# A recommendation tower on one core: plain fp32 field products on 32-row strips, weights loaded once, and gathers without a pause between them

## The reference

```
e = jnp.stack([tbl_0[ids[:, 0]], ..., tbl_38[ids[:, 38]]], axis=1)   # 512 x 39 x 32
z = jnp.einsum('bpc,apc,bpa->bp', e[:, ROW, :], w, e[:, COL, :])     # 512 x 741 pairs
h = jnp.concatenate([z, dense_ctx], axis=1)                          # 512 x 757
h = jnp.maximum(h @ W_top1 + b_top1, 0.0)                            # 512 wide
h = jnp.maximum(h @ W_top2 + b_top2, 0.0)                            # 256 wide
y = h @ W_top3
```

## Time and profile before

| | |
|---|---|
| time, median of 3 runs | 290.9 us (290.44 to 292.17) |
| profiled execution: span from first to last instruction | 285.0 us |
| the median over that span | 5.9 us more |
| busy: PE, DVE, POOL, ACT | 198.8, 146.6, 134.8, 97.5 us |
| mean granted TensorE clock | 0.844 of full speed |

### The profile page before, as it was taken

How to read it: one execution, slowest core, us unless ns; L and a number is a source line. 1 busy time by engine, 2 the same in 40 slices (tenths; PEclk the granted TensorE clock), 3 DMA queues, 4 the chain that set the end, 5 groups by cost and what they waited for, 6 DMA issues and landing times.

```text
span 285.0 us, 2687 instructions
## 1 busy us (share of the span) xinstructions
PE 198.8 (70%) x974; PEld 73.5 (26%) x974; DVE 146.6 (51%) x115; ACT 97.5 (34%) x142; POOL 134.8 (47%) x134
## 2 busy tenths in 40 slices
PE   0048668453212277738798197699899999999996
PEld 0012223000000033213333032243333334344341
DVE  0353794101000027824794266389599779898230
ACT  2516899300000047830540071037127127110032
POOL 7774767777777300776587887200042015007000
PEclk9999797755555559795999669599999999999999
DMA  4869779700000003997266018148715846450000
GB/s 134 257 210 300 285 177 212 164 16 13 14 13 13 9 0 74 300 207 148 50 158 166 12 41 183 41 96 167 167 33 118 183 98 129 98 121 1 0 2 0
DMA packets 11352, 31.40 MB, mean 110 GB/s; under 512 B 3230, under 2 KB 7098, under 8 KB 10379
## 3 DMA queue, kind: packets, MB, share of 16 engines
q1 hardware_dynamic: 7882, 29.45, 42.1%
q0 software_dynamic: 3456, 1.78, 3.5%
HBM read 12.34 MB, written 0.00 MB: 43 GB/s over the span
## 4 chain that ended last, share of the span: by engine, by line
PE 51%; issue 18%; DMA 9%; DVE 7%; SPq 6%; another core or an unknown queue 4%; ACT 3%; DVEq 0%; ACTq 0%
PE t_ps L719 16%; PE z_ps L735 15%; PE z_ps L688 9%; DMA mlp<-tbl 6%; PE side_ps L750 5%; DMA wring<-w_lo 4%; DVE prod L658 3%; SPq L425 2%; PE t_ps L777 2%; DVE prod L629 2%; SPq L431 1%; SPq L475 1%; PE t_ps L765 1%; PE t_ps L770 1%
## 5 line engine op out<-in xcount | busy, mean ns | idle before, releaser
L658 DVE TENSOR_TENSOR prod<-t_ps,eT 128x1536 f32<-128x1536 f32 (+2 forms) x70 | 109.9, 1600 | 79.3 <-PE t_ps L719 49.7
L514 POOL DMA_INDIRECT gathered<-tbl,ids_sb x108 | 104.9, 971 | 53.5 <-issue 31.4
L719 PE MATMUL t_ps<-stack,wring 128*128 128x512 f32 x210 | 72.9, 464 | 12.2 <-issue 6.7
L735 PE MATMUL z_ps<-prod,sel 128*32 128x512 f32 x380 | 57.5, 645 | 4.6 <-issue 4.6
L719 PEld LDWEIGHTS t_ps<-stack,wring 128*128 128x128 f32 x210 | 38.3, 205 | 65.8 <-issue 39.5
L688 PE MATMUL z_ps<-prod,room 125*32 125x512 bf16 x72 | 21.0, 534 | 34.1 <-issue 33.3
L528 POOL TENSOR_TENSOR room<-room,w_hi 128x512 f32<-128x512 f32 x3 | 3.9, 1286 | 66.3 <-ACT w_hi L603 66.3
L629 DVE TENSOR_SCALAR prod<-mlp,slice_rows 125x2048 bf16<-125x2048 f16 x18 | 14.8, 856 | 23.0 <-remote 23.0
L587 ACT ACTIVATE stack<-hi_lo 32x512 fp32r<-32x512 f32 x39 | 24.6, 629 | 2.6 <-issue 1.2
L580 ACT ACTIVATE stack<-eT 32x512 fp32r<-32x512 f32 x39 | 24.4, 625 | 1.0 <-PE t_ps L719 0.7
L750 PE MATMUL side_ps<-room,mlp 128*128 128x512 f32 x32 | 18.4, 660 | 7.7 <-ACT eT L567 7.6
(11 more groups left out here) (49 smaller groups left out, 113.5 us busy)
## 6 DMA issues: line engine op xcount, KB each, us to landing
wring<-w_hi SPq DMA_DIRECT2D x30, 224.0 KB
wring<-w_lo SPq DMA_DIRECT2D x30, 224.0 KB
stack<-stack SPq DMA_DIRECT2D x9, 512.0 KB
w_lo<-wst SPq DMA_DIRECT2D x4, 896.0 KB, 15.2
eT<-hot_ids SPq DMA_DIRECT2D x3, 1024.0 KB
gathered<-tbl,ids_sb POOLq DMA_INDIRECT x108
mlp<-w SPq DMA_DIRECT2D x1, 1536.0 KB
mlp<-tbl SPq DMA_DIRECT2D x12, 125.0 KB
```

The costliest lines, as they stand in the source:

```text
L514: pool.indirect_dma_start(gathered[:, n % GATHER_BUFS, b, K * r:K * r + K], None, tables[f], bass.IndirectOffsetOnAxis(ap=ids_sb[:, F * b ...
L658: dve.tensor_tensor(prod[:, g % XSLOTS, 0:n, :], t_ps[g % 2][:, 0:n, :], field, ALU.mult).then_inc(multiplied, 1)
L719: mm = pe.matmul(t_ps[g % 2][:, i, :], wring[:, c % WSLOTS, passes % WCHUNK, :].bitcast(F32R), stack[:, J % STACKS, src - G * J, :].bitcas ...
L735: mm = pe.matmul(z_ps[K * (u % G):K * (u % G) + K, :], sel[:, u // G, :], prod[:, g % XSLOTS, t - TILE_BASE[g], :], start=(u < G), stop=(u ...
```

## The change

- **Tiles in plain fp32.** No high and low parts, no `stack`, no weight ring. A tile of field r of block J is a full fp32 product that uses only the 32 rows of that field, `w_sb[rows, w_tile, :]` by `eT[rows, J, :]`; the four tiles of a *quad* (J, I) use the four row strips 0, 32, 64 and 96 of the array and four PSUM banks. Within a block (the diagonal) two tiles of 64 rows each are used, for the last block one of 128. The count stays at 190 tiles, now in 55 quads and 100 *pairs* of one or two tiles; DVE multiplies a pair at a time. `t` has three slots of two banks, `prod` six slots.
- **Weights loaded once.** `w_sb` holds all of the weights; SP issues all its loads at the start, the table blocks first, then `w_sb` block by block, then the network's weights.
- **Byte-wise lookups.** The twelve looked-up fields are now blocks 0, 1 and 2. The upper 16 bits of each fp32 entry are read in place as bf16; ACT turns the two lower bytes into bf16 (two copies a block). The products of the upper half and of the two lower bytes go to two banks, and ACT writes them back as the two halves of the fp32 word. There are still 12 products a slice and 24 slices. The ids are spread over the partitions by 12 small PE products instead of three 1 MB loads. `hot` has six buffers of its own.
- **Gathers.** Seven buffers, one for each gathered block (3 to 9), so POOL issues all 108 without a wait or other work in between.
- The early part of the first layer takes 5 of the 6 z blocks in three rounds (20 full products), the sixth comes last.

```diff
+LOOKED = [0, 1, 2]
+DIAGONAL = [[(0, 1), (0, 2), (1, 3)], [(2, 1), (3, 0), (3, 2)]]
+for _J in range(NBLK):
+    QUADS += [(_J, _I, FIELDS_IN[_J]) for _I in range(_J)]
+    QUADS.append((_J, _J, 2 if FIELDS_IN[_J] == G else 1))
+PAIRS = [(q, i, min(2, QUADS[q][2] - i)) for q in range(NQUAD) for i in range(0, QUADS[q][2], 2)]
+TSLOTS = 3
+XSLOTS = 6
+ROUNDS = [[0, 1], [2, 3], [4]]
+SEL_LAG = 2
+KEEP_LEAD = 3
...
+    steps += [("ids", 0), ("lower", 0), ("ids", 1), ("look", 0, 0, 3), ("lower", 1), ("ids", 2), ("look", 0, 3, 8),
+              ("keep", 0), ("lower", 2), ("look", 1, 0, 8), ("keep", 1), ("look", 2, 0, 3), ("quad", 0), ("look", 2, 3, 8), ("keep", 2),
+              ("quad", 1)]
...
-        gathered = sb("gathered", [P, GATHER_BUFS, NCHUNK, P])
+        gathered = {J: sb(f"gathered{J}", [P, NCHUNK, P]) for J in GATHERED}
+        w_sb = sb("w_sb", [P, WTILES, P])
+        upper = [tab[h].bitcast(BF16) for h in range(NHOT)]
+        bytes_of = [tab[h].bitcast(U8) for h in range(NHOT)]
...
-                if n >= GATHER_BUFS:
-                    pool.wait_ge(turned, n - GATHER_BUFS + 1)
...
+            for J, r in fields:
+                f = BLOCKS[J][r]
+                for b in range(NCHUNK):
+                    pool.indirect_dma_start(
+                        gathered[J][:, b, K * r:K * r + K], None, tables[f],
...
+                elif step[0] == "lower":
+                    h = step[1]
+                    act.wait_ge(tab_in[h], 16 * len(tab_pieces))
+                    for i in range(2):
+                        act.activation(lower[i][h][0:HP, :, :], bytes_of[h][0:HP, :, 1 - i::4], ACT.Copy,
+                                       scale=256.0 if i == 0 else 1.0).then_inc(lower_made, 1)
...
+                        act.activation(words.bitcast(BF16)[:, 1::2], look_ps[h][0], ACT.Copy)
+                        act.activation(words.bitcast(U16)[:, 0::2], look_ps[h][1], ACT.Copy).then_inc(eT_made, 1)
...
+                        if p >= TSLOTS:
+                            pe.wait_ge(multiplied, p - TSLOTS + 1)
+                        for i in range(first, first + n):
+                            rows = source_rows(q, i)
+                            mm = pe.matmul(ps[:, 2 * (p % TSLOTS) + i - first, :], w_sb[rows, w_tile(q), :],
+                                           eT[rows, J, :], start=True, stop=True)
+                        mm.then_inc(t_made, 1)
```

More of the change, by code:

```diff
@@ L77 @@
+FIRST_TILE = [TILE_BASE[q] + i for q, i, _ in PAIRS]
+PAIRS_THROUGH = [sum(1 for p in PAIRS if p[0] <= q) for q in range(NQUAD)]
+TSLOTS = 3
+XSLOTS = 6
 ZTILES = P // G
 ZM = ZTILES // G
[L81 to L109, removed]
@@ L126, with sources @@
[L126 to L133, removed]
-SEL_LAG = 2
+NZ = -(-NTILE // ZTILES)
+ROUNDS = [[0, 1], [2, 3], [4]]
+SEL_LAG = 2
+KEEP_LEAD = 3
+PACE = 2
+Z_LAG = 2
+def sources(q):
+    J, I, n = QUADS[q]
+    if I < J:
+        return [[(r, c) for c in range(G)] for r in range(n)]
+    if FIELDS_IN[J] == G:
+        return DIAGONAL
+    return [LAST_DIAGONAL]
@@ new lines, in source_rows, with w_tile, pair_of, z_row @@
+def source_rows(q, i):
+    J, I, n = QUADS[q]
+    if I < J:
+        return slice(K * i, K * i + K)
+    return slice(P // n * i, P // n * i + P // n)
+def w_tile(q):
+    J, I, _ = QUADS[q]
+    return W_BASE[J] + I
+def pair_of(a, b):
+    i, j = min(a, b), max(a, b)
+    return i * (2 * F - i - 1) // 2 + (j - i - 1)
+def z_row(t, r):
+    return (t // ZTILES) * P + (t % G) * K + (t % ZTILES // G) * G + r
+_taken = {(TILE_BASE[q] + i, c) for q in range(NQUAD) for i, tile in enumerate(sources(q)) for _, c in tile}
@@ L137, in plan @@
+_free = [z_row(t, c) for t in range(NTILE) for c in range(G) if (t, c) not in _taken]
+DENSE_ROWS = []
+while len(DENSE_ROWS) < NDENSE // 2:
+    _a, _b = _free[:2]
+    if _a // P == _b // P:
+        DENSE_ROWS.append((min(_a, _b), abs(_a - _b)))
+    _free = _free[2 if _a // P == _b // P else 1:]
+DENSE_BLOCKS = sorted({first // P for first, _ in DENSE_ROWS})
 def plan():
     steps, done = [], 0
-    early = [(m, n, i) for n in range(len(ROUNDS)) for m in range(M1) for i in range(len(ROUNDS[n]))]
@@ L156, in plan @@
[L156 to L161, removed]
+    early = [(m, n) for n in range(len(ROUNDS)) for m in range(M1)]
+    since = 0
     def sums(upto, exact):
@@ L184, in plan @@
[L184 to L204, removed]
@@ L205, in plan, with there @@
-    sums(NGROUP - 2, True)
-    steps += [("early", *e) for e in early]
[L207 to L212, removed]
+    def there(zb):
+        names = [s[:2] for s in steps]
+        return ("z", zb) in names and sum(s[0] == "quad" for s in names[names.index(("z", zb)):]) > Z_LAG
@@ new lines, in plan @@
+    steps += [("ids", 0), ("lower", 0), ("ids", 1), ("look", 0, 0, 3), ("lower", 1), ("ids", 2), ("look", 0, 3, 8),
+              ("keep", 0), ("lower", 2), ("look", 1, 0, 8), ("keep", 1), ("look", 2, 0, 3), ("quad", 0), ("look", 2, 3, 8), ("keep", 2),
+              ("quad", 1)]
+    for q in range(2, NQUAD):
+        J = QUADS[q][0]
+        steps.append(("quad", q))
+        since += 1
+        for T in GATHERED:
+            if q == FIRST_QUAD[T] - KEEP_LEAD:
+                steps.append(("keep", T))
+        near = any(0 < FIRST_QUAD[T] - KEEP_LEAD - q <= 1 for T in GATHERED)
+        if early and since >= PACE and not near and all(there(zb) for zb in ROUNDS[early[0][1]]):
+            steps.append(("early", *early.pop(0)))
+            since = 0
+        sums(q - SEL_LAG, False)
+        sums(q - SEL_LAG - 1, True)
@@ L215 @@
+    sums(NQUAD - 2, True)
+    steps += [("early", *e) for e in early]
+    sums(NQUAD - 1, True)
+    return steps
 PLAN = plan()
-LAST_FIRST = [M1 - 1] + list(range(M1 - 1))
-assert NGROUP % 2 == 0
-SPLITS = [s[1:] for s in PLAN if s[0] == "split"]
 TURNS = [s[1] for s in PLAN if s[0] == "keep"]
-assert all([s[1] for s in PLAN if s[0] == part] == TURNS for part in ("halve", "stack"))
+SUMS = [s for s in PLAN if s[0] == "sums"]
+EARLY = [s[1:] for s in PLAN if s[0] == "early"]
+SUMS_THROUGH = [next(i + 1 for i, s in enumerate(SUMS) if s[1] + s[2] >= FIRST_TILE[p] + PAIRS[p][2])
+                for p in range(NPAIR)]
@@ L223, in turns @@
+assert sorted(TURNS) == list(range(NBLK))
+assert [T for T in TURNS if T in LOOKED] == LOOKED and [T for T in TURNS if T in GATHERED] == GATHERED
 def turns(J):
     return TURNS.index(J) + 1
[L228 to L245, removed]
 def lay_out_weights(w, W_top1):
-    wst = np.zeros((NWCOL, G, K, WCHUNK, G, K), w.dtype)
+    wst = np.zeros((G, K, WTILES, G, K), w.dtype)
     w1 = np.zeros((NZ * P, H1), W_top1.dtype)
[L256 to L268, removed]
+    for q, (J, I, n) in enumerate(QUADS):
+        for i, tile in enumerate(sources(q)):
+            for src, c in tile:
+                a, b = BLOCKS[J][src], BLOCKS[I][c]
+                block = w[:, pair_of(a, b), :]
+                wst[src, :, w_tile(q), c, :] = block if a > b else block.T
+                w1[z_row(TILE_BASE[q] + i, c)] = W_top1[pair_of(a, b)]
@@ L347, in dlrm_tower @@
+        tab_in = [sem(f"tab_in{h}") for h in range(NHOT)]
+        w_in = [sem(f"w_in{J}") for J in range(NBLK)]
         mlp_in = sem("mlp_in")
@@ L668, in _ @@
+            for m in range(M1):
+                dve.wait_ge(h1_made, m + 1)
+                if m == 0:
+                    dve.wait_ge(early_kept, len(EARLY))
+                    dve.wait_ge(early_added, M1 * (len(ROUNDS) - 1))
+                    dve.wait_ge(summed, len(SUMS))
+                dve.tensor_tensor(h1_sum[m], h1_ps[m], h_early[0][:, m, :], ALU.add).then_inc(h1_added, 1)
         @block.tensor
         def _(pe):
-            passes = 0
-            side_used = []
+            side_used = [(eT_made, turns(2))]
```

590 lines of the change are left out of this document (221 added, 369 removed).

## The result

The change made the kernel slower: 329.7 us (329.51 to 330.06) against 291.5 (290.44 to 292.21), a ratio of 1.132 (95% interval 1.125 to 1.138). The forecast was 211, the range 197 to 300. The answer depends on the chip, and that is what the experiments are about: repeated on a chip where the kernel before takes 292.1 us the change takes 330.8, and on one where the kernel before takes 222.1 it takes 210.4 (a single run). On chips of the first kind one execution in seven of the kernel before was 2 to 3% quicker than the median (284.6 and 285.3 us), which would make the change look worse, not better.

The account below looks back on a forecast made before the run. Before, PE bounds 186 to 262 us; an earlier slow stretch has no known cause. Block 8's turn at 131, 55.6 of work behind it, 3 of DVE stalls, 15.7 of tail: span 205, plus 5.9: 211 us, range 197 to 300.

Parts of the forecast that it names:

- the lookups end at about 33: Start of the kernel: 24 lookup slices at 0.83 us each on PE, ending at about 33 us instead of 103.
- the drag: Lookups of the kernel before, 46.9 to 97 us: PE starts only 53 matmuls, though nobody the trace shows is waited for.
- R2: PE drags whenever gathers run without a break; 305 us if it begins inside the lookups; chance 0.27.
- the mild episode: Kernel before, at 154 us: a turned block done by 154.63 is taken by ACT only at 162.44.
- B: Rival in the experiments' expectations: the lookups are slow by themselves and gathers don't matter; no chance given.
- A: Rival in the experiments' expectations: any long run of gathers drags PE, at whatever pitch; no chance given.
- C: Rival in the experiments' expectations: gathers slow only the lookups, not the tiles; no chance given.
- D: Rival in the experiments' expectations: PE drags only where gathers run while the DMA is otherwise quiet; no chance given.
- the forecast's own case: Whole kernel: lookups at pace, then PE's work and waits for gathered blocks; 211 us, own range 198 to 228, chance 0.42.
- R3: Tiles: row strips don't overlap, so a quad costs 3.44 us instead of 1.15; time 292 us, chance 0.07.
- R1: Lookups: one stretch drags as before, so tiles start at 85 to 90 us; 228 to 262 us, chance 0.16.
- theory Q: From the experiments: each gather holds for 1.40 us something PE's instructions need; issued each 1.25 us, a backlog grows.

## Why the prediction was wrong, point by point

**What failed** is the first term of the sum, "the lookups end at about 33": it let 24 slices run at 0.83 us each with the drag at nothing, and on the measured chip they ended at 169.1. Behind it stands the weighing of the rivals: R2, "PE drags whenever gathers run without a break", came true and was given 0.27, against it "at 40 to 46.9 the lookups ran at pace beside gathers" and "If it were gathers alone, those would have dragged too". That reasoning took the cause for something that acts at once. The runs show an effect that sets in later: in the change PE ran at pace through its first 12 gathers or so and then dragged, and in the kernel before through the first 6 of the run of 44, to 47 us. The other sentence against R2, on 103 to 129 us, overlooked that PE stood still there without a cause that the profile names, 5.51 us up to 128.99, with POOL gathering:

```profile
128.99 2.50 PE L719 MATMUL t_ps<-stack,wring 128*128 128x512 f32 x5 [5.51 <-issue]
160.42 0.94 POOL L514 DMA_INDIRECT gathered<-tbl,ids_sb  x1 [0.30 <-issue]
```

And the mild episode didn't end 6 us behind its gathers, as the prediction has it: the last of its 12 starts at 160.42, and ACT takes the block at 162.44. An end 2 us behind 12 gathers and 8 behind 44 was the hint that the number counts. R2's price was short as well. It let the drag end at 142 with 10 us of lookups left; it ended at 154, some 13 of the 24 slices were left, and the lookups ended at 169.1. Tiles and tail then took 159.1 against 151 in the sum (132 + 19); the half of the gathers shows that this is their work alone (190.7 less the 31.6 at which its lookups end: 159.1). 169.1 + 159.1 is the span of 328.2, where R2 had 303.

**The mechanism, as far as it is shown.** Shown: on chips with the drag its end follows the number of gathers, by 1.40 us a gather (154 for 108, twice; 132 for 92; 102 for 44 from 40.3), and so comes 15, 13 and 8 us behind the start of the last one; in the middle of the change's drag PE gets one instruction through per 1.38 us. The slowing is gradual: in 20 to 30 us of the change it was one per 0.5, and once the gathers are over it eases again (16 in 140 to 154). That three doses lie on one line speaks for a backlog and against B; A stays open, since no run changed the pitch there. C doesn't fit the kernel before, where tiles stand still too. Short runs fit only in part: for the 12 gathers from 146.68 the reckoning gives 163.5 (ACT at 162.44), but for the 16 from 113.61 it gives 136.0, and PE works again from 128.99, at half clock. D stays open: PE was slowed less at 46.9 to 57 us, with DMA at 0.81, than at 57 to 97 with 0.09. The granted clock doesn't seem to be what makes the drag long: 2.2 of each 2.8 us are gaps between matmuls of 0.59, and two of the four executions of the first result have a mean of 1.00 on record and took 329.5 us, the other two 0.792 and 329.9 and 330.1. Not tried on such a chip: paced gathers, late gathers, and gathers of 64 rows: all of these ran on chips without the drag. Whether gathers 1.44 us apart leave PE alone there, whether the hold goes by rows, and what it is that gathers and PE's instructions share, stays open, and so does what differs between the chips.

**Where the forecast's own case held.** On chip 3, without the drag, the forecast's case can be read step by step in one run. The lookups end at 30.9 (forecast 33). A quad takes 1.07 (1.15 in the sum, bounds 0.99 and 3.44): row strips overlap like the column strips of the earlier trace rows, so R3 is refuted. The Trainium skill ("TensorE: Matmul & The Clock Gate", "Part 3: Packing small matmuls — row/col tiling") gives 3.07 times the rate; worked out from that figure, an estimate of 1.12, and the trace agrees within 5%. Sums 1.00, DVE 1.217 and 0.683 a product (1.24 and 0.69). PE waits for blocks 5 and 6 as forecast, comes to block 7's turn at 106.1 with no wait (forecast: there at 103, waiting to 107) and to block 8's at 130.1 (131). The tail takes 15.2 (15.7), the tiles behind block 8's turn 63.3 (58.6): behind DVE a quad often takes 1.27 or 1.45 instead of 1.07. So the span is 208.6 against 205. That the time, 210.4, is so near to 211 is partly luck: from span to time it was 1.8 us there, not 5.9. Every execution whose span is on record has 1.5 to 1.8; the 5.9 must have come of setting the median beside the span of a quicker execution. The lookups (2 us less) and the tiles (5 more) were off against each other as well. R1, a single stretch of the lookups dragging, doesn't occur in any trace.

**What the change is worth**, then, depends on the chip: 210 against 222 where PE doesn't drag (one run); 330 against 292 where it does. By theory Q that is because its gathers are one run of 108 and its lookups stand beside them, where before POOL's waits for buffers and its other work cut them into runs of 16, 4, 44, 16, 4, 12 and 12, so that a backlog could drain between.

## What to carry to other kernels

A stretch in which an engine is slow and waits for nobody is the first thing to explain before forecasting an edit near it; here it was worth more than all of the edit's counted work. When a suspected cause seems to act at one time and not at another, ask whether it accumulates: divide the distance from the first event to the end of the effect by the number of events, in every episode. It gives 1.40 for the long runs here and fits the short ones only in part. And a kernel whose "before" differs by 30% between chips has to be compared on both kinds.

## What the runs showed of the hardware that wasn't expected

- The same kernel takes 221 to 224 us on seven chips and 291 to 292 on two, and beside the first run of the change. In the drag TensorE is granted half of its clock (0.50 in 57 to 97 us, 0.50 in 60 to 140 in the change); the change's lookups on chip 3 run at 1.00.
- On the chips that take 291, PE slows beside long runs of indirect gathers 1.25 us apart, from the 6th to 12th gather until about 1.40 us times their number after the first, and down to one instruction per 1.38 us in runs of 92 and 108.
- Completions are seen late in the drag: ACT took the first block of the lookups at 155.21, after a wait of 132.01 us, though the last of its 96 products started at 81.0. In the second trace of the change it is 124.3 against 40.3, and with 92 gathers 129.4 against 44.7.
- Gathers with a memset between them came 1.44 us apart in quiet and about 1.7 beside DVE's comparisons, 1.25 and 1.33 without it.
